# Ranks of tokens by a running sum on VectorE and three products, in place of nine products on TensorE

## The chip, the cores and the metric

The kernel runs on one core of a Trainium2 chip. The metric is device time in microseconds for one execution, the median of several runs; before the change it is 1121.83 us (three runs, 1119.72 to 1124.03).

## The reference

The input x is 128 graphs of 128 nodes with 128 features. Four layers follow one another, each a residual on a layer norm of x:

```python
x = x + gnn0(layernorm(x))   # h = x@W; softmax over neighbours of leaky_relu(s1_i + s2_j); elu(att @ h)
x = x + ffn0(layernorm(x))   # 8 experts, the best 2 of each token, softmax weights, gelu
x = x + gnn1(layernorm(x))   # as gnn0 with other weights; relu
x = x + ffn1(layernorm(x))   # 32 experts, the best 1 of each token, relu
```

For the two expert layers the tokens must be grouped. The first has 28 pairs of experts, the second 32 experts. Each token (a node of a graph) needs a row number: the start of its class, plus the tokens of that class in earlier batches, plus its rank in its own batch, which is how many tokens stand before it in the same class.

## The kernel before

There are two attention passes (l = 0 and 1), each followed by a mixture stage that reads the grouped tokens. A pass works in groups of G = 4 graphs, 32 groups (NG), as a software pipeline of turns `i`: in turn i group i is loaded and scaled, group i-1 gets its products h and scores, i-2 its weights, i-3 and i-4 the attention product, residual and statistics, i-5 its routing logits. The order of work in each engine is written out by hand in that engine's `graph_layer(l)`; engines meet in semaphores. VectorE's `link(op)` waits for the end of op before the next instruction; without it the next may start while op ends.

Routing and ranks are done for two groups at once. This is a batch b: eight graphs, w = 8 columns of tokens, 16 batches in each pass. On VectorE a turn runs, in this order: statistics of the coming x (first pass only), `weights` (L715, L722), in odd batches' turns `places`, `logits` (L754), then in the turn of a batch `first0`, `second0`, `pair0` (first pass, 28 pair codes) or `route1` (second pass, 32 experts), then `scores` (L742 the row maximum, L743 `nm`), `residual` (L732, L733 or L735, which write `staged`) and statistics. So in one turn of two the routing stands between `weights` and `scores`, and in the other turn `places` does.

The routing ends with a one-hot `oh` in bf16, of 8 x 28 = 224 or 8 x 32 = 256 elements a partition (L793, L800), with token columns outside and classes inside. A partition is a node number. The rank of a token is the count of ones of its class in all earlier graphs of the batch plus those on lower partitions of its own graph. TensorE makes that in the bank `SM`: one product with the strict triangle `below` (L1338), and eight with all ones (L1340), the q-th of which adds graph q to all the columns from q+1 on. The ninth column of the result is the batch's total. Then TensorE transposes `staged` (L1262), and makes h (L1279) and the scores (L1287, L1291, L1292) of a later group. In `places` (L809 to L829) VectorE adds the running `base`, multiplies by the one-hot and sums to the row numbers `dst`. GpSimd scatters the rows with them by indirect DMAs (L507), eight for each batch, and also computes the inverse deviations (L459, L469, L473). ScalarE's turn is: copies of `pt` (L1154) and `xT`, eight exponentials (L1117, L1118) that need `nm`, then the activations on the attention product, `x1T`, `xs_` and `hg`.

At the end of a pass a table of tiles is made from the counts, and the mixture stage starts when all scatters have landed.

Of the kernel before, what the change touches and what calls it, by code (L numbers as in the profile page):

```python
# [6 lines left out]
BF16 = mybir.dt.bfloat16  # L7
I32 = mybir.dt.int32
U32 = mybir.dt.uint32
ALU = mybir.AluOpType  # L10
# [3 lines left out]
P = 128  # L14
NGRAPH = 128
G = 4
# [71 lines left out]
def program(nc, x, adj, W_0, a_0, gamma, beta, Wr, br, W1_0, b1_0, W2_0, b2_0,  # L88
            W_1, a_1, rw, rb, W1_1, b1_1, W2_1, b2_1, out):
    with ExitStack() as ctx:  # L90
        def sb(name, shape, dt=F32):
            return ctx.enter_context(nc.sbuf_tensor(name, shape, dt))
# [29 lines left out]
        below = sb("below", [P, P], BF16)  # L122
        cmat = sb("cmat", [P, P])
        eps = sb("eps", [P, 2, 2 * G])
        eps1 = sb("eps1", [P, G])
# [83 lines left out]
        th = sb("th", [P, RB])  # L209
        ka = sb("ka", [P, RB])  # L210
        oh = sb("oh", [P, RB * NB[0]], BF16)
        base = [sb(f"base{s}", [P, E1]) for s in range(2)]
        pos = sb("pos", [P, RB * NB[0]])
        posoh = sb("posoh", [P, RB * NB[0]])
# [213 lines left out]
        def _(pool):  # L428
# [62 lines left out]
            pool.memset(onesb[:, :], 1.0).then_inc(sem("onesb"), 1)  # L491
            pool.memset(pad[:, :], 0.0).then_inc(sem("pad"), 1)
            pool.wait_ge(sem("onesb"), 1)
            pool.affine_select(out=below[:, :], in_=onesb[:, :], compare_op=ALU.is_gt, fill=0.0, base=0,
                               pattern=[[1, P]], channel_multiplier=-1)
            pool.wait_ge(sem("pad"), 1)
            pool.memset(pad[:, ID:ID + 1].bitcast(I32), NOWHERE).then_inc(sem("pad"), 1)

# [68 lines left out]
        def _(dve):  # L567
# [192 lines left out]
            def rows(t, k, E):  # L760
                return t[:, 0:E].unsqueeze(1).broadcast_to([P, k * G, E])

            def best(src, k, E, r, m, key):

                a, c = ge3(la, k, E), ge3(lk, k, E)
                link(dve.reduce_max(m[:, 0:k * G], src, AX.X))
                link(dve.tensor_tensor(a, src, wide(m, k, E), ALU.is_ge))
                link(dve.tensor_tensor(c, a, rows(r, k, E), ALU.mult))
                link(dve.reduce_max(key[:, 0:k * G], c, AX.X))
# [14 lines left out]
            def pair0(b, k):  # L784
                w = k * G
                mark(dve.tensor_tensor(ka[:, 0:w], k1[:, 0:w], k2[:, 0:w], ALU.add))
                dve.tensor_tensor(sd[:, 0:w], k1[:, 0:w], k2[:, 0:w], ALU.is_gt)
                after(dve, "th", b - 1)
                mark(dve.tensor_tensor(hd[:, 0:w], ma[:, 0:w], mb[:, 0:w], ALU.subtract))
                settled()  # L790
                dve.scalar_tensor_tensor(hd[:, 0:w], sd[:, 0:w], 0.5, hd[:, 0:w], ALU.subtract, ALU.mult).then_inc(sem("hd"), 1)
                after(dve, "rank_ps", b - 1)
                dve.tensor_tensor(ge3(oh, k, NB[0]), rows(codes, k, NB[0]), wide(ka, k, NB[0]), ALU.is_equal).then_inc(sem("oh"), 1)  # L793

            def route1(b, k):
                E = E1
                link(dve.tensor_tensor(ge3(lg, k, E), ge3(lgb, k, E), rows(cl[1], k, E), ALU.add))
                best(ge3(lg, k, E), k, E, rev, ma, k1)
                after(dve, "rank_ps", b - 1)
                dve.tensor_tensor(ge3(oh, k, E), rows(rev, k, E), wide(k1, k, E), ALU.is_equal).then_inc(sem("oh"), 1)  # L800

            def places(b):
                g, k = ORDER[b]
                l, w = g // NG, k * G
                B = NB[l]
                after(dve, "rank_ps", b)
                r = SM[:, 0:(w + 1) * B].rearrange("p (g e) -> p g e", e=B)
                old, new = base[b % 2], base[(b + 1) % 2]
                dve.tensor_tensor(new[:, 0:B], old[:, 0:B], r[:, w, :], ALU.add).then_inc(sem("base"), 1)  # L809
                dve.tensor_tensor(ge3(pos, k, B), r[:, 0:w, :], old[:, 0:B].unsqueeze(1).broadcast_to([P, w, B]),  # L810
                                  ALU.add).then_inc(sem("ranks_read"), 1)
                if l == 0:
                    after(dve, "th", b)
# [7 lines left out]
                        dve.tensor_scalar(staged[:, s:s + run, :, WHI], t, -0.5, 0.5, ALU.mult, ALU.add)  # L821
                        h += run
                after(dve, "ranks_read", b)
                link(dve.tensor_tensor(ge3(posoh, k, B), ge3(pos, k, B), ge3(oh, k, B), ALU.mult))
                if b >= ND:
                    for m in range(ORDER[b - ND][0], sum(ORDER[b - ND])):
                        dve.wait_ge(sem(f"scattered{m % NS}"), 16 * G * (m // NS + 1))
# [390 lines left out]
        def _(pe):  # L1218
# [46 lines left out]
            def graph_layer(l):  # L1265
                E = (E0, E1)[l]
                B = NB[l]
                for i in range(NG + 8):
# [62 lines left out]
                    if i in PART[l][2]:  # L1331
                        b = PART[l][2][i]
                        k = ORDER[b][1]
                        w = k * G
                        after(pe, "oh", b)
                        o = oh[:, 0:w * B].rearrange("p (g e) -> p g e", e=B)
                        r = SM[:, 0:(w + 1) * B].rearrange("p (g e) -> p g e", e=B)
# [115 lines left out]
```

## Time and profile before

| | us |
|---|---|
| median of 3 runs | 1121.83 |
| profiled execution, its own time | 1121.34 |
| its span, first to last instruction | 1119.6 |
| TensorE busy | 888.0 |
| VectorE busy | 794.6 |
| GpSimd busy | 761.7 |
| ScalarE busy | 699.1 |

The passes and the mixture stages follow one another, so a busy share has to be read within a stage. PEclk is the granted share of TensorE's full clock: 1.00 is 2.4 GHz, 0.50 is 1.2 GHz, and a value between is a mean over the stretch. A row of windows gives the stretch and its length, then for each engine the busy microseconds and, as (x105), the number of instructions. In rows of the timeline the first number is the start, the second the duration from the first to the last of the instructions merged in the row (their pipelined ends included), and the bracket gives how long the engine stood idle before and what ended it.

### The profile page before, as it was taken

Reading aid. Unit: us, or ns where it says so; the run is one execution under the profiler, and the core shown is the slowest. Engines: PE = TensorE matmul, PEld = TensorE weight load, DVE = VectorE, ACT = ScalarE, POOL = GpSimd, SP = SyncE. Lnnn points to the kernel's source line nnn. Section 1 sums busy time; section 2 is a strip of 40 time slices with the busy share of each in tenths; the row PEclk is TensorE's granted clock in tenths of the full one; section 3 lists DMA queues with packets and bytes.
Section 4 is the critical chain, followed back from the end, with each engine's and each line's share of the span. In section 5 each row is a group of like instructions: output and inputs, shape, how many; then the busy total and the mean of one; then the engine's idle time right before and its main releaser. Section 6 shows DMA issues by size and latency. Waiting matters only on the chain. (4 is left out here: it accounts for less than half of the span.)

```text
span 1119.6 us, 26953 instructions
## 1 busy us (share of the span) xinstructions
PE 888.0 (79%) x6709; PEld 797.9 (71%) x6709; DVE 794.6 (71%) x3521; ACT 699.1 (62%) x2364; POOL 761.7 (68%) x975
## 2 busy tenths in 40 slices
PE   4788988988618999999999759999999518878810
PEld 3567777877618999999999747888888406666610
DVE  7779899888846999999999716888888823422310
ACT  2799899888504665566556459999998306653300
POOL 3327777677762887877888811787878846777776
PEclk9899899889758999999999979999999659985555
DMA  8323432221157888887878321223221145433311
GB/s 197 54 83 123 141 123 85 70 58 47 35 114 198 210 208 209 210 208 206 213 204 207 94 67 29 74 84 85 79 78 50 41 104 146 117 99 104 90 33 38
DMA packets 144935, 129.21 MB, mean 115 GB/s; under 512 B 26552, under 2 KB 116541, under 8 KB 144785
## 3 DMA queue, kind: packets, MB, share of 16 engines
q1 hardware_dynamic: 124144, 91.94, 33.2%
q0 software_dynamic: 17760, 34.20, 9.0%
q10 hardware_dynamic: 2880, 1.35, 0.6%
q8 instruction: 60, 0.98, 0.4%
q14 instruction: 91, 0.74, 0.3%
HBM read 82.74 MB, written 47.48 MB: 116 GB/s over the span
## 5 line engine op out<-in xcount | busy, mean ns | idle before, releaser
L507 POOL DMA_INDIRECT xs<-staged,dst x256 | 258.1, 1008 | 77.2 <-issue 68.6
L1168 ACT ACTIVATE hT<-bank,wt 128x128 f32<-128x128 f32 x620 | 177.3, 368 | 130.9 <-PE bank L1383 114.6
L538 POOL DMA_INDIRECT x2d<-ob,xi x155 | 161.0, 1038 | 43.0 <-issue 28.7
L560 POOL DMA_INDIRECT out<-oq,xq x144 | 142.9, 992 | 58.4 <-issue 42.7
L1369 PE MATMUL bank<-xnT,wt 128*128 128x128 f32 x1240 | 166.0, 277 | 0.0
L1383 PE MATMUL bank<-w2s,hT 128*128 x1240 | 164.0, 275 | 0.7 <-DVE ob L1041 0.5
L1369 PEld LDWEIGHTS bank<-xnT,wt 128*128 128x128 f32 x1240 | 152.8, 194 | 0.1
L1383 PEld LDWEIGHTS bank<-w2s,hT 128*128 128x128 f32 x1240 | 150.9, 192 | 1.0 <-issue 1.0
L1117 ACT ACTIVATE p<-bank,nm 128x128 f32<-128x128 f32 x256 | 103.2, 403 | 27.0 <-DVE nm L743 27.0
L1118 ACT ACTIVATE p<-bank,nm 128x128 f32<-128x128 f32 x256 | 104.8, 410 | 0.0
L1131 ACT ACTIVATE rl<-bank,rinv 128x128 f32<-128x128 f32 x256 | 97.1, 453 | 3.1 <-DVE staged L735 3.1
L1068 DVE SCALAR_TENSOR_TENSOR oq<-bank,xq 128x512 f32<-128x512 f32 x36 | 24.9, 692 | 103.0 <-PE bank L1414 57.3
L715 DVE SCALAR_TENSOR_TENSOR pm<-p 128x128 f32<-128x128 f32 x256 | 61.7, 288 | 46.0 <-ACT p L1118 44.7
L1303 PEld LDWEIGHTS bank<-hg,pt 128*128 128x128 f32 x512 | 68.3, 195 | 29.0 <-issue 29.0
L1279 PE MATMUL bank<-wcat,xT 128*128 128x128 f32 x512 | 78.4, 303 | 7.5 <-DVE wa L644 3.9
L1291 PEld LDWEIGHTS bank<-wa,xT 128*128 128x128 f32 x512 | 75.7, 212 | 6.1 <-issue 2.4
L1279 PEld LDWEIGHTS bank<-wcat,xT 128*128 128x128 f32 x512 | 71.5, 216 | 9.6 <-ACT xT L1106 4.9
L1210 ACT ACTIVATE xnqT<-bank 128x512 f32<-128x512 f32 x36 | 21.5, 596 | 89.1 <-PE bank L1262 89.1
L1291 PE MATMUL bank<-wa,xT 128*128 128x128 f32 x512 | 74.6, 294 | 0.0
L1328 PEld LDWEIGHTS bank<-wrc,x1T 128*128 128x128 f32 x512 | 64.7, 198 | 7.7 <-ACT x1T L1136 5.5
L1328 PE MATMUL bank<-wrc,x1T 128*128 128x8 f32 (+1 forms) x512 | 64.8, 262 | 6.4 <-ACT x1T L1136 3.3
L742 DVE TENSOR_REDUCE nmax<-bank 128x4 f32<-128x512 f32 x64 | 43.8, 685 | 35.7 <-PE bank L1292 35.7
(250 smaller groups left out, 2203.3 us busy)
## 6 DMA issues: line engine op xcount, KB each, us to landing
wt<-wpd SPq DMA_DIRECT2D x155, 258.0 KB
xi<-xs SPq DMA_DIRECT2D x155, 66.0 KB
xq<-xs SPq DMA_DIRECT2D x144, 66.0 KB
xb<-x2d SPq DMA_DIRECT2D x32, 258.0 KB, 3.1
xb<-in_x SPq DMA_DIRECT2D x32, 256.0 KB, 3.9
wpd<-w1c SPq DMA_DIRECT2D x56, 129.0 KB
xs<-staged,dst POOLq DMA_INDIRECT x256, 2.5
x2d<-ob,xi POOLq DMA_INDIRECT x155
```

The lines of the kernel that those rows point to most:

```text
L507: pool.indirect_dma_start(out=xs[l], out_offset=bass.IndirectOffsetOnAxis(ap=dst[b % ND][:, c:c + 1], axis=0), in_=stag[s][:, q, 0:ROW], i ...
L538: pool.indirect_dma_start(out=x2d, out_offset=bass.IndirectOffsetOnAxis(ap=xi[t % NXI][:, ID:ID + 1].bitcast(U32), axis=0), in_=ob[:, t % ...
L560: pool.indirect_dma_start(out=orow, out_offset=bass.IndirectOffsetOnAxis(ap=xq[j % NXQ][:, q, ID:ID + 1].bitcast(U32), axis=0), in_=oq[j % ...
L1117: act.activation(p1[:, q, :], S[:, q, :], ACT.Exp, bias=nm[:, q:q + 1])
L1118: last = act.activation(p2[:, q, :], S[:, q, :], ACT.Exp, bias=nm[:, q:q + 1], scale=SLOPE[l])
L1131: last = act.activation(rl[:, q, :], z, ACT.Relu, scale=rinv[m % 3][:, q:q + 1])
L1168: last = act.activation(hT[t % 2][:, j, :], HID[t % 2][:, j, :], ACT.Gelu, bias=wt[t % NW][:, c:c + 1])
L1279: last = pe.matmul(HB[:, c], xT[:, c], wcat[l][:, :], start=(q == 0), stop=(q == G - 1), skip_group_check=True)
L1291: pe.matmul(S[:, c], xT[:, c], wa1[l][:, :], start=False, stop=False, skip_group_check=True)
L1328: last = pe.matmul(SM[:, LOGITS[l] + q * E:LOGITS[l] + (q + 1) * E], x1T[:, q * P:(q + 1) * P], wrc[l][:, :], start=(q == 0), stop=(q == G ...
L1369: last = pe.matmul(HID[t % 2][:, j, :], wt[t % NW][:, c:c + P], xnT[t % 2][:, :], start=(j == 0), stop=(j == 3), skip_group_check=True)
L1383: last = pe.matmul(to, hT[t % 2][:, 2 * h + c, :], w2s[:, bass.ds(e + c * E0 * P, P)], start=(h == 0 and c == 0), stop=(h == 1 and c == 1) ...
```

## The change

The one-hot is written with classes outside and the eight graphs inside. VectorE then makes a running sum over it, `state = gate * state + oh`, where `gate` is 0 at the first graph of every class and 1 elsewhere: `upto_` holds for each class and graph the ones on that partition in this graph and all earlier ones. One product with all ones sums that over the partitions; one with `lessone` (0 for lower partitions, -1 for the token's own and higher ones) takes away the tokens of its own graph at and above its partition; a third, over the last graph of each class, is the total. TensorE waits for "prefix", which the scan signals, in place of "oh". `places` reads the ranks and the one-hot with graphs eight elements apart. On GpSimd the constants change: `lessone` and `gate` in place of `below`, with three more memsets.

```diff
+            pool.memset(onesb[:, :], 1.0)
+            pool.memset(gate[:, :], 1.0)
+            pool.memset(lessone[:, :], 0.0).then_inc(sem("onesb"), 1)
...
-            pool.affine_select(out=below[:, :], in_=onesb[:, :], compare_op=ALU.is_gt, fill=0.0, base=0,
+            pool.affine_select(out=lessone[:, :], in_=lessone[:, :], compare_op=ALU.is_gt, fill=-1.0, base=0,
                                pattern=[[1, P]], channel_multiplier=-1)
+            pool.memset(gate[:, :].rearrange("p (e g) -> p e g", g=2 * G)[:, :, 0], 0.0).then_inc(sem("gate"), 1)
...
+            def eg3(t, k, E):
+                return t[:, 0:k * G * E].rearrange("p (e g) -> p g e", e=E)
+
+            def prefix(b, k, E):
+                if b == 0:
+                    dve.wait_ge(sem("gate"), 1)
+                dve.tensor_tensor_scan(upto_[:, 0:k * G * E], gate[:, 0:k * G * E], oh[:, 0:k * G * E], 0.0, ALU.mult,
+                                       ALU.add).then_inc(sem("prefix"), 1)
...
-                dve.tensor_tensor(ge3(oh, k, NB[0]), rows(codes, k, NB[0]), wide(ka, k, NB[0]), ALU.is_equal).then_inc(sem("oh"), 1)
+                link(dve.tensor_tensor(eg3(oh, k, NB[0]), rows(codes, k, NB[0]), wide(ka, k, NB[0]), ALU.is_equal))
+                prefix(b, k, NB[0])
...
-                dve.tensor_tensor(ge3(oh, k, E), rows(rev, k, E), wide(k1, k, E), ALU.is_equal).then_inc(sem("oh"), 1)
+                link(dve.tensor_tensor(eg3(oh, k, E), rows(rev, k, E), wide(k1, k, E), ALU.is_equal))
+                prefix(b, k, E)
...
-                r = SM[:, 0:(w + 1) * B].rearrange("p (g e) -> p g e", e=B)
+                r = SM[:, 0:w * B].rearrange("p (e g) -> p g e", e=B)
...
-                link(dve.tensor_tensor(ge3(posoh, k, B), ge3(pos, k, B), ge3(oh, k, B), ALU.mult))
+                link(dve.tensor_tensor(ge3(posoh, k, B), ge3(pos, k, B), eg3(oh, k, B), ALU.mult))
...
-                        after(pe, "oh", b)
...
-                        pe.matmul(r[:, 0:w, :], below[:, :], o, start=True, stop=False, skip_group_check=True)
-                        for q in range(w):
-                            last = pe.matmul(r[:, q + 1:w + 1, :], onesb[:, :], o[:, q:q + 1, :].broadcast_to([P, w - q, B]),
-                                             start=False, stop=(q == w - 1), skip_group_check=True)
-                        last.then_inc(sem("rank_ps"), 1)
+                        after(pe, "prefix", b)
+                        n_ = w * B
+                        ends = upto_[:, 0:n_].rearrange("p (e g) -> p e g", g=w)[:, :, w - 1]
+                        pe.matmul(SM[:, 0:n_], lessone[:, :], oh[:, 0:n_], start=True, stop=False, skip_group_check=True)
+                        pe.matmul(SM[:, 0:n_], onesb[:, :], upto_[:, 0:n_], start=False, stop=False, skip_group_check=True)
+                        pe.matmul(SM[:, n_:n_ + B], onesb[:, :], ends, start=False, stop=True,
+                                  skip_group_check=True).then_inc(sem("rank_ps"), 1)
```

## Rows read from the trace of the kernel before

**Rows 1.** The page: busy time of each engine over the span.

```profile
PE 888.0 (79%) x6709; PEld 797.9 (71%) x6709; DVE 794.6 (71%) x3521; ACT 699.1 (62%) x2364; POOL 761.7 (68%) x975
```

**Rows 2.** Windows: twelve batches of the first pass, twelve of the second.

```profile
core 0: us, PE busy (x) PEld busy (x) DVE busy (x) ACT busy (x) POOL busy (x), PEclk, DMA share, GB/s
76.52:276.86 200.34, 173.01 (x1246) 152.96 (x1245) 179.58 (x886) 178.65 (x593) 144.15 (x166) 0.91 0.31 93
697.17:860.59 163.42, 155.78 (x1239) 138.01 (x1238) 139.92 (x625) 151.66 (x481) 127.09 (x165) 1.00 0.27 75
```

**Rows 3.** Windows, one batch each, from one-hot to next one-hot.

```profile
76.52:92.50 15.98, 14.20 (x113) 12.41 (x113) 14.97 (x75) 15.98 (x54) 8.96 (x11) 1.00 0.38 118
...
125.16:143.16 18.00, 15.43 (x102) 13.41 (x101) 15.05 (x75) 14.52 (x50) 13.10 (x15) 0.81 0.39 119
143.16:158.77 15.61, 13.28 (x108) 11.80 (x107) 14.86 (x75) 14.96 (x50) 11.74 (x14) 1.00 0.44 138
158.77:175.37 16.60, 14.13 (x103) 12.46 (x102) 15.07 (x76) 14.55 (x50) 13.55 (x15) 0.90 0.41 129
...
192.19:209.14 16.95, 14.69 (x105) 13.03 (x104) 15.08 (x76) 14.82 (x50) 12.07 (x14) 0.90 0.22 64
...
778.88:792.49 13.61, 12.97 (x105) 11.49 (x105) 11.66 (x52) 12.63 (x41) 10.86 (x15) 1.00 0.30 81
```

**Rows 4.** Timeline of VectorE in the first pass.

```profile
209.14 0.38 DVE L793 TENSOR_TENSOR oh<-codes,ka 128x224 bf16<-128x224 f32 x1
209.44 0.68 DVE L742 TENSOR_REDUCE nmax<-bank 128x4 f32<-128x512 f32 x1
...
216.91 0.69 DVE L742 TENSOR_REDUCE nmax<-bank 128x4 f32<-128x512 f32 x1 [0.80 <-PE bank L1292]
```

**Rows 5.** Timeline of TensorE in the first pass.

```profile
209.58 0.27 PE L1338 MATMUL bank<-oh,below 128*128 128x224 bf16 x1
209.69 0.61 PE L1340 MATMUL bank<-oh,onesb 128*128 128x224 bf16 x8
211.71 1.00 PE L1262 MATMUL bank<-ident,staged 128*128 128x128 f32 x4 [1.42 <-DVE staged L733]
```

**Rows 6.** VectorE's groups by form: count, busy us, mean ns, idle before.

```profile
L767 DVE TENSOR_TENSOR la<-lg,ma 128x256 f32<-128x256 f32 x16 | 6.8, 425 | 0.5
L766 DVE TENSOR_REDUCE ma<-lg 128x8 f32<-128x256 f32 x16 | 6.7, 420 | 0.5
...
L767 DVE TENSOR_TENSOR la<-lg,ma 128x64 f32<-128x64 f32 x16 | 3.6, 224 | 0.5
```

**Rows 7.** Timeline of VectorE in the second pass.

```profile
788.83 0.29 DVE L715 SCALAR_TENSOR_TENSOR pm<-p 128x128 f32<-128x128 f32 x1 [1.09 <-ACT p L1118]
...
792.04 0.42 DVE L769 TENSOR_REDUCE k<-lk 128x8 f32<-128x256 f32 x1
792.49 0.42 DVE L800 TENSOR_TENSOR oh<-rev,k 128x256 bf16<-128x256 f32 x1
792.84 0.68 DVE L742 TENSOR_REDUCE nmax<-bank 128x4 f32<-128x512 f32 x1
```

**Rows 8.** Timelines of TensorE and ScalarE in the second pass.

```profile
792.97 0.28 PE L1338 MATMUL bank<-oh,below 128*128 128x256 bf16 x1
794.38 0.66 PE L1262 MATMUL bank<-ident,staged 128*128 128x128 f32 x4 [0.62 <-DVE staged L735]
785.64 0.60 ACT L1154 ACTIVATE pt<-bank 128x512 f32<-128x512 f32 x1 [0.17 <-PE bank L1262]
793.75 0.37 ACT L1117 ACTIVATE p<-bank,nm 128x128 f32<-128x128 f32 x1 [0.80 <-DVE nm L743]
```

**Rows 9.** Timelines at the ends of the passes, and GpSimd's waits (us, times, longest).

```profile
296.64 0.20 POOL L459 TENSOR_TENSOR ve<-var,eps 128x4 f32<-128x4 f32 x1 [0.29 <-DVE var L619]
...
POOL xs L507 <- DVE dst L829: 8.1, 13, 1.5
...
912.50 0.96 POOL L507 DMA_INDIRECT xs<-staged,dst  x1 [0.30 <-issue]
```

More of the change, by code:

```diff
@@ L121, in program @@
         onesb = sb("onesb", [P, P], BF16)
-        below = sb("below", [P, P], BF16)
+        lessone = sb("lessone", [P, P], BF16)
+        gate = sb("gate", [P, RB // 2 * E1], BF16)
         cmat = sb("cmat", [P, P])
@@ L211, in program @@
         oh = sb("oh", [P, RB * NB[0]], BF16)
+        upto_ = sb("upto_", [P, RB * NB[0]], BF16)
         base = [sb(f"base{s}", [P, E1]) for s in range(2)]
@@ L490, in _ @@
             last.then_inc(sem("iotas"), 1)
-            pool.memset(onesb[:, :], 1.0).then_inc(sem("onesb"), 1)
+            pool.memset(onesb[:, :], 1.0)
+            pool.memset(gate[:, :], 1.0)
+            pool.memset(lessone[:, :], 0.0).then_inc(sem("onesb"), 1)
             pool.memset(pad[:, :], 0.0).then_inc(sem("pad"), 1)
             pool.wait_ge(sem("onesb"), 1)
-            pool.affine_select(out=below[:, :], in_=onesb[:, :], compare_op=ALU.is_gt, fill=0.0, base=0,
+            pool.affine_select(out=lessone[:, :], in_=lessone[:, :], compare_op=ALU.is_gt, fill=-1.0, base=0,
                                pattern=[[1, P]], channel_multiplier=-1)
+            pool.memset(gate[:, :].rearrange("p (e g) -> p e g", g=2 * G)[:, :, 0], 0.0).then_inc(sem("gate"), 1)
             pool.wait_ge(sem("pad"), 1)
@@ L806, in places @@
                 after(dve, "rank_ps", b)
-                r = SM[:, 0:(w + 1) * B].rearrange("p (g e) -> p g e", e=B)
+                r = SM[:, 0:w * B].rearrange("p (e g) -> p g e", e=B)
                 old, new = base[b % 2], base[(b + 1) % 2]
-                dve.tensor_tensor(new[:, 0:B], old[:, 0:B], r[:, w, :], ALU.add).then_inc(sem("base"), 1)
-                dve.tensor_tensor(ge3(pos, k, B), r[:, 0:w, :], old[:, 0:B].unsqueeze(1).broadcast_to([P, w, B]),
+                dve.tensor_tensor(new[:, 0:B], old[:, 0:B], SM[:, w * B:(w + 1) * B], ALU.add).then_inc(sem("base"), 1)
+                dve.tensor_tensor(ge3(pos, k, B), r, old[:, 0:B].unsqueeze(1).broadcast_to([P, w, B]),
                                   ALU.add).then_inc(sem("ranks_read"), 1)
@@ L1334, in graph_layer @@
                         w = k * G
-                        after(pe, "oh", b)
-                        o = oh[:, 0:w * B].rearrange("p (g e) -> p g e", e=B)
-                        r = SM[:, 0:(w + 1) * B].rearrange("p (g e) -> p g e", e=B)
-                        pe.matmul(r[:, 0:w, :], below[:, :], o, start=True, stop=False, skip_group_check=True)
-                        for q in range(w):
-                            last = pe.matmul(r[:, q + 1:w + 1, :], onesb[:, :], o[:, q:q + 1, :].broadcast_to([P, w - q, B]),
-                                             start=False, stop=(q == w - 1), skip_group_check=True)
-                        last.then_inc(sem("rank_ps"), 1)
+                        after(pe, "prefix", b)
[5 more added lines that the diff above has]
+                                  skip_group_check=True).then_inc(sem("rank_ps"), 1)
                     if 0 <= i - 4 < NG:
```

## The prediction

> **What bounds the kernel now.** The page's busy line first [rows 1]: no engine is above 79% of the span, so a share over everything decides nothing. The windows by stage then show where the edit lives [rows 2]. In the first attention pass, from 76.5 to 276.9 us, VectorE is busy 90% (179.58 of 200.34), ScalarE 89%, TensorE 86%. In the second pass's full part, 697.2 to 860.6 us, TensorE is busy 95%, ScalarE 93%, VectorE 86%. Read by shares alone, the second pass looks like TensorE's, and taking products from TensorE looks like a gain. The order in time says something else.
>
> A batch is eight graphs, two turns of the pipeline, 16 batches in each pass. In the second pass every batch takes 13.6 us (the last of [rows 3]). Follow one turn round [rows 7, 8]: ScalarE ends the exponentials, and VectorE, which had waited 1.09 us for them, starts L715 at 788.83. From there it never stops: masked weights, logits, `route1`, the one-hot at 792.49, the row maximum at 792.84, `nm`. ScalarE has waited 0.80 us for that `nm`, and runs from 793.75 until the next such L715. From 788.83 to 793.75 the loop is VectorE's, 4.9 us; the other 8.7 of the batch's 13.6 us are ScalarE's. TensorE stands beside it: it starts the rank products at 792.97, and then waits 0.62 us for `staged`, which VectorE writes after `nm`. So the products fill time in which TensorE would wait.
>
> In the first pass a batch takes 15.61 to 15.98 us where the granted clock is 1.00 (three batches of twelve), 16.60 to 16.95 us in eight and 18.00 us in one [rows 3]. The rank products start at 209.58 and TensorE then waits 1.42 us for `staged` [rows 5]. VectorE comes to that `staged` straight through routing, one-hot and row maximum; behind it, TensorE's work at half clock makes VectorE wait 0.80 us in the next turn's L742 [rows 4]. Where the clock is full, VectorE alone sets the batch.
>
> **Removed: TensorE's products.** Columns per batch fall from 224 + (8+7+...+1) x 28 = 1232 to 224 + 224 + 28 = 476 in the first pass, from 1408 to 544 in the second. One column is 1/2.4 ns at full clock; [rows 5] agree, the nine products taking 0.72 us for 1232 columns with the last one's tail (0.51 us without). That is 0.32 and 0.36 us less a batch. I book it at nothing: the waits of 1.42 and 0.62 us stand right behind. If that cover were gone the edit would give back 0.32 x 14 + 0.36 x 13 = 9.2 us.
>
> **Added: a completed one-hot and a running sum on VectorE.** (a) The one-hot is now followed by a wait for its end. Unlinked, a 256-element instruction starts its successor 0.35 us later (792.49 to 792.84); linked, 0.46 us (792.04 to 792.49). Plus 0.11 us. At 224 elements the unlinked pitch is 0.30 (209.14 to 209.44), so 0.41 linked [rows 4, 7]. (b) The scan over 224 or 256 elements. No row shows one. From below: it costs what a tensor_tensor of that size does, a pitch of 0.30 or 0.35 us. From above: each element waits for two dependent operations (multiply by the gate, then add), so an element takes two steps in place of one. From 64 to 256 elements an instruction grows from 224 to 425 ns, 1.04 ns an element [rows 6]; the second step adds 0.23 us (224) or 0.27 us (256): pitches of 0.53 and 0.61 us. I take the upper. The reduction, nearest of all rows, does feed each result into the next and runs at one element a step (420 ns at 256), but it has one operation in its loop, the scan two.
>
> Together VectorE does 0.64 us more a batch in the first pass and 0.73 us in the second, before `nm`, `staged` and everything queued behind. TensorE waits longer behind "prefix": its queue holds the transposes of `staged`, which are late anyway by the same amount; ScalarE waits longer for `nm`.
>
> The Trainium skill, page "DVE: opcode table, instruction layouts, handler registers and perf-mode slots", section "Datapath and trigger behaviour", says that the built-in running sum sends its result back to an earlier stage and runs at half throughput. That speaks against this change; by it the sum is the upper one, and by the reduction's row the lower, 6.7 us less. No run here shows it yet.
>
> (c) Edits at nothing. `places` now reads PSUM and the one-hot eight elements apart (L810, L824). If each element took two steps this would add 0.46 to 0.54 us, but in the second pass 1.09 us of waiting for ScalarE follows in that turn, and in the first the 0.80 us wait for TensorE; it shows only in batches at full clock. Writing the one-hot at that stride (L793, L800) is on the path; 0 from below, 0.23 or 0.27 us from above. Every row of a wide instruction here has contiguous output and none is nearer to one end; I take 0, since it still writes one element a step, and keep the other end for the range. GpSimd's three more memsets of at most 256 elements come once, some 65 us ahead of the first batch; at VectorE's 0.4 us for 256 elements they would be 1 us of a stretch in which GpSimd mostly waits: 0. The rows before the pass, the mixture stages and all DMAs are untouched.
>
> **How many batches count.** At each pass's end GpSimd's scatters take over. In the first, its last wait for VectorE's statistics is the 0.29 us at 296.64, after the one-hot of the fourteenth batch; from there it runs without waiting for VectorE until the last scatter. In the second, GpSimd waits for `dst` 13 times, the last for the thirteenth batch, then works through to 912.50 [rows 9]. What VectorE loses in later batches is hidden behind that queue. In the last batch of a pass nothing but the products stands between one-hot and `places`, and the edit could gain; that too is hidden. So 14 x 0.64 + 13 x 0.73 = 9.0 + 9.5 = 18.5 us.
>
> **TensorE's clock.** In the first pass it fell to half in nine of the twelve batches from 76.52 to 276.86 us; batches without a fall average 15.8 us and all twelve 16.7 us [rows 2, 3], so the falls cost 0.9 us a batch (200.34 / 12 - 15.8). What stood before them is the 1.42 us gap, with little but narrow products ahead of it. In the second pass, gap 0.62 us, the mean is 1.00 over twelve batches [rows 2]. After the change TensorE runs out of work at 793.0 as now, gets the prefix about 793.65 (792.49 + 0.46 + 0.69), works about 0.3 us, and waits for `staged` until 795.1: gaps of 0.65 and 1.15 us with a short burst between, together more than the 1.42 us that went with falls. A fall costs more there, since TensorE's way from `staged` to the transposed weights ends with ScalarE waiting 0.17 us for it [rows 8]: 3 to 4 us of work at half clock is up to 1.7 us, of which I count 1.1. I take half of 13 batches: 7 us. In the first pass the gaps grow to 0.6 and 1.9 us; if nearly every batch falls and one in six falls twice (18.00 us, plus 2.2), the mean is 1.3 in place of 0.9: 0.4 x 12 = 5 us. Both are estimates from these rows.
>
> The Trainium skill, "TensorE: Matmul & The Clock Gate", section "Part 1: The HAM clock gate", says that the default is the throttled state and that activity releases it. The trace agrees at the 0.90 rows, and by that rule taking work from TensorE beside a wait costs twice.
>
> **The sum** against the profiled execution, 1121.34 us (span 1119.6; the median is 1121.83): 18.5 + 7 + 5 = 30.5, so 1152 us.
>
> **Rivals.** *Work only* (chance 0.22): the clock behaves as now, 1121.3 + 18.5 = 1140 us. For: in the first pass 1.4 us gaps also went by without a fall (three batches). *Full-rate sum* (0.14): the scan streams like the reduction; 14 x 0.41 + 13 x 0.46 = 11.7, so 1133 us without clock losses, 1143 with most of them. *More than one loss* (0.13): strided writes at two steps (14 x 0.23 + 13 x 0.27 = 6.7) or falls in nearly every batch of the second pass (13 x 1.1 = 14 in place of 7): 1159 to 1166 us. *The other side* (0.05): TensorE is the bound after all. It holds if the products end later than `staged`, that is if the 0.62 us wait is only apparent and VectorE's additions fit in its own 0.32 and 1.09 us waits: then 1121.3 - 9.2 = 1112 us, or about 1121 if both cancel. Against it: the added work stands after those waits, not before them, and ScalarE's 0.80 us wait is for VectorE. My forecast, 0.46, has its own range of 1144 to 1159 us. A measurement of this kernel tells about 0.5% (5.6 us) from no change; only the last rival, 0.02 faster and 0.03 same, stays inside or below that, and with it 0.01 more of the full-rate case. The range for 8 in 10 reaches from just below the full-rate case to the larger losses, 1131 to 1165 us.
>
> **What the profile after would show.** The scan's row: near 620 and 690 ns (upper) or 384 and 424 ns (lower). From the one-hot's start to L742's: 0.94 and 1.07 us in place of 0.30 and 0.35. A batch of the second pass at 14.3 us where the clock is 1.00 and near 15.5 where it fell; TensorE's two gaps; L1117's wait for `nm` longer, L715's 1.09 us unchanged or shorter. GpSimd's wait for `dst` grows by 0.7 us in each of 13 batches. The mixture stages keep their length. The prediction is wrong if TensorE's granted clock stays 1.00 in the second pass, if the scan takes as long as a tensor_tensor, or if the batch does not grow by what VectorE gained.

## The result, and the profile after

The changed kernel takes 1197.78 us (median of four runs, 1194.77 to 1200.60) against 1122.63 us for the kernel before in the same comparison (1119.72 to 1124.03): 1.0668 times, 95% interval 1.0644 to 1.0692. The direction was forecast, the size was not: 30 us were expected and 75 came, and the forecast's range, up to 1165 us, does not hold it. The profiled execution took 1198.69 us (span 1196.7, mean granted clock 0.845), 77.1 us of span more than before.

The page of the changed kernel: span, busy time by engine, and the granted clock in forty slices.

```profile
span 1196.7 us, 26605 instructions
...
PE 918.9 (77%) x6517; PEld 819.0 (68%) x6517; DVE 848.7 (71%) x3553; ACT 697.8 (58%) x2364; POOL 769.3 (64%) x978
...
PEclk9888988888657999999999699988998755797555
```

VectorE is busy 54 us longer than in [rows 1]. TensorE is busy 31 us longer too, though it has 192 products fewer, with a mean granted clock of 0.845 where it was 0.881. In the slices of the first pass (the third to the twelfth) the granted clock is mostly 0.8; a 9 stands for anything from 0.90 up, so the second pass is read from its windows below.

Its groups by form in the first pass (100 to 280 us; count, busy us, mean ns, idle before), then both forms of the one-hot and of the sum from a query by tile (min/median/max ns):

```profile
L807 DVE TENSOR_TENSOR oh<-codes,ka 128x224 bf16<-128x224 f32 x9 | 10.3, 1143 | 0.0
L840 DVE TENSOR_TENSOR posoh<-pos,oh 128x224 f32<-128x224 f32 x10 | 5.7, 566 | 0.0
L774 DVE TENSOR_TENSOR_SCAN upto_<-gate,oh 128x224 bf16<-128x224 bf16 x9 | 5.6, 625 | 0.3
L826 DVE TENSOR_TENSOR pos<-bank,base 128x224 f32<-128x224 f32 x10 | 3.8, 383 | 0.0
```

```profile
L774 DVE TENSOR_TENSOR_SCAN upto_<-gate,oh x32: 624/658/692, 76.5 to 964.6; 128x224 bf16<-128x224 bf16 x16, 128x256 bf16<-128x256 bf16 x16
...
L815 DVE TENSOR_TENSOR oh<-rev,k x16: 1290/1294/1298, 726.4 to 963.3; 128x256 bf16<-128x256 f32 x16
```

The sum takes 624 and 692 ns, the forecast's upper price (near 620 and 690). The one-hot is the surprise: 1144 ns in place of 384 and 1294 in place of 424 [rows 4, 7]. Its elements and its arithmetic are the same; what changed is that neighbours in the loop are now written 8 elements apart. That is 0.76 and 0.87 us a batch, where the prediction had 0 and, as its upper bound, 0.23 and 0.27.

Windows of one batch each, two of the first pass and two of the second (start:end, length, busy time and count of PE, PEld, DVE, ACT, POOL, granted clock, DMA share, GB/s):

```profile
150.05:169.35 19.30, 15.42 (x99) 13.36 (x98) 16.60 (x76) 14.76 (x50) 12.64 (x14) 0.82 0.36 112
169.35:187.58 18.23, 14.34 (x99) 12.50 (x98) 16.64 (x76) 14.77 (x50) 12.20 (x14) 0.91 0.38 118
827.31:844.16 16.85, 14.32 (x100) 12.33 (x99) 13.50 (x53) 12.61 (x41) 11.07 (x14) 0.90 0.23 65
844.16:859.40 15.24, 12.71 (x100) 11.10 (x99) 13.47 (x54) 12.66 (x41) 9.86 (x13) 1.00 0.26 66
```

Set these beside [rows 3]. The last row is the batch without a fall: 15.24 against 13.61 + 0.73 (link and sum) + 0.87 (one-hot) = 15.21. The row above it is what eleven of the twelve full batches look like: a fall of the clock, a stretch at half clock, adds 1.6 us to them. In the first pass the two rows alternate, one fall and two, and none is free of one.

The timeline of one routing in the second pass, VectorE and TensorE (start, us, what it waited for):

```profile
793.62 1.30 DVE L815 TENSOR_TENSOR oh<-rev,k 128x256 bf16<-128x256 f32 x1
...
794.95 0.69 DVE L774 TENSOR_TENSOR_SCAN upto_<-gate,oh 128x256 bf16<-128x256 bf16 x1
795.55 0.67 DVE L747 TENSOR_REDUCE nmax<-bank 128x4 f32<-128x512 f32 x1
...
795.69 0.28 PE L1354 MATMUL bank<-oh,lessone 128*128 128x256 bf16 x1 [1.60 <-DVE upto_ L774]
...
796.45 0.37 ACT L1133 ACTIVATE p<-bank,nm 128x128 f32<-128x128 f32 x1 [2.42 <-DVE nm L748]
...
797.08 0.66 PE L1278 MATMUL bank<-ident,staged 128*128 128x128 f32 x4 [0.94 <-DVE staged L740]
```

From the one-hot's start to the row maximum it is 1.93 us where [rows 7] have 0.35. ScalarE's wait for `nm` grew from 0.80 [rows 8] to 2.42 us, by the 1.6 us that VectorE gained. TensorE has two gaps, 1.60 and 0.94 us with 0.4 us of work between, where it had one of 0.62.

GpSimd's waits in the second pass (720 to 990 us; us, times, longest):

```profile
POOL xs L512 <- DVE dst L845: 21.9, 14, 1.7
```

[Rows 9] had 8.1 us.

**Where the 77.1 us lie.** The starts of the first one-hot of each pass are 75.31 and 726.40 us (76.52 and 697.17 before), the starts of the last scatters 358.95 and 984.15 us (331.41 and 912.50). So the first pass grew by 28.7 us (283.6 after, 254.9 before), the stretch between by 1.7, the second pass by 42.4 (257.8 after, 215.3 before), the last stage by 5.5, and 1.2 came off the start.

### The profile page after: what moved, and what is told of

Its sections match the earlier page's. It is cut to its first block and busy times, and to the rows that moved or that the text cites. A ratio compares the mean times of both kernels' runs of the same rounds, so it can differ in the third digit from the quotient of the medians.

```text
span 1196.7 us, 26605 instructions
## 1 busy us (share of the span) xinstructions
PE 918.9 (77%) x6517; PEld 819.0 (68%) x6517; DVE 848.7 (71%) x3553; ACT 697.8 (58%) x2364; POOL 769.3 (64%) x978
## 3 DMA queue, kind: packets, MB, share of 16 engines
q10 hardware_dynamic: 2880, 1.35, 0.6%
## 5 line engine op out<-in xcount | busy, mean ns | idle before, releaser
L512 POOL DMA_INDIRECT xs<-staged,dst x256 | 265.1, 1036 | 90.9 <-issue 67.8
L565 POOL DMA_INDIRECT out<-oq,xq x144 | 144.6, 1004 | 62.2 <-issue 42.4
L1133 ACT ACTIVATE p<-bank,nm 128x128 f32<-128x128 f32 x256 | 101.8, 398 | 64.8 <-DVE nm L748 64.7
L1134 ACT ACTIVATE p<-bank,nm 128x128 f32<-128x128 f32 x256 | 103.4, 404 | 0.0
L1295 PE MATMUL bank<-wcat,xT 128*128 128x128 f32 x512 | 90.2, 335 | 6.6 <-ACT xT L1122 3.6
L1307 PEld LDWEIGHTS bank<-wa,xT 128*128 128x128 f32 x512 | 85.3, 235 | 7.8 <-issue 2.4
L1295 PEld LDWEIGHTS bank<-wcat,xT 128*128 128x128 f32 x512 | 83.0, 246 | 8.7 <-ACT xT L1122 4.9
L1307 PE MATMUL bank<-wa,xT 128*128 128x128 f32 x512 | 82.8, 315 | 0.0
L1278 PE MATMUL bank<-ident,staged 128*128 128x128 f32 x256 | 51.7, 336 | 36.7 <-DVE staged L738 23.7
L461 POOL TENSOR_TENSOR ve<-var,eps 128x8 f32<-128x8 f32 (+1 forms) x38 | 8.6, 226 | 107.3 <-DVE var L624 107.3
L1170 ACT ACTIVATE pt<-bank 128x512 f32<-128x512 f32 x64 | 42.2, 660 | 56.1 <-PE bank L1278 56.0
```

Of the source, the lines that this page charges most:

```text
L512: pool.indirect_dma_start(out=xs[l], out_offset=bass.IndirectOffsetOnAxis(ap=dst[b % ND][:, c:c + 1], axis=0), in_=stag[s][:, q, 0:ROW], i ...
L565: pool.indirect_dma_start(out=orow, out_offset=bass.IndirectOffsetOnAxis(ap=xq[j % NXQ][:, q, ID:ID + 1].bitcast(U32), axis=0), in_=oq[j % ...
L1133: act.activation(p1[:, q, :], S[:, q, :], ACT.Exp, bias=nm[:, q:q + 1])
L1134: last = act.activation(p2[:, q, :], S[:, q, :], ACT.Exp, bias=nm[:, q:q + 1], scale=SLOPE[l])
L1295: last = pe.matmul(HB[:, c], xT[:, c], wcat[l][:, :], start=(q == 0), stop=(q == G - 1), skip_group_check=True)
L1307: pe.matmul(S[:, c], xT[:, c], wa1[l][:, :], start=False, stop=False, skip_group_check=True)
```

## The experiments

Four of them (`after_fill`, `probe_strides`, `e1_late`, `b_fill_order`) ran on a chip on which the kernel before takes 1177.13 us, with longer mixture stages (in `b_fill_order` 380 us between the passes and 249 behind the last scatter, where the kernel before has 366 and 207); from these only ratios, batches, lengths of the passes and durations are used.

**1. The one-hot in memory order.** All of the change, but the loop of the one-hot runs as its result lies in memory; its inputs are broadcasts either way.

```diff
-link(dve.tensor_tensor(eg3(oh, k, E), rows(rev, k, E), wide(k1, k, E), ALU.is_equal))
+link(dve.tensor_tensor(eg(oh, k, E), deep(rev, k, E), wided(k1, k, E), ALU.is_equal))
+# eg:    [0:k*G*E] as "p (e g) -> p e g";  deep: class value, broadcast over g;  wided: key, broadcast over e
```

> The changed kernel with one thing undone: the one-hot is computed in the order in which it lies in memory (class by class, the eight graphs innermost), so each write is next to the last; its values and its place are the same. Theory A (the stride of the 16-bit write is what I priced at 0): the one-hot falls from 1144 and 1294 ns to 384 and 424 ns, VectorE's path by 0.76 and 0.87 us a batch, 14 x 0.76 + 13 x 0.87 = 22 us: 1176 us if the clock falls as often as in the changed kernel, 1152 us if in half of the second pass's batches, 1140 us if as in the kernel before. Rival B (the operands with a broadcast in the middle, or the waits, make it slow, not the stride): the one-hot stays above 1 us and the time near 1198 us.

1159.87 us (1156.99 to 1160.48), 1.0306 times the kernel before (1.0273 to 1.0340). The one-hot is back at 384 and 424 ns. Of twelve batches in the second pass, seven are like the first of these windows and five like the second:

```profile
726.28:740.65 14.37, 12.71 (x100) 11.11 (x99) 12.61 (x53) 12.67 (x41) 9.46 (x13) 1.00 0.28 71
740.65:756.63 15.98, 14.28 (x100) 12.55 (x99) 12.64 (x54) 12.60 (x41) 12.42 (x16) 0.89 0.25 72
```

This is the kernel that the prediction described: 14.3 us forecast for a batch at full clock, a fall in about half of the batches. Writing without the stride gives back 38 us, half of the whole loss; that holds the write's own time and the falls that it drew. Still, the time is 8 us above the 1152 expected for this case. Of these, 5 lie in the last stage (212.1 us behind the last scatter, 207.1 before), which had been booked at nothing.

**2. Products that nobody reads, behind the prefix.** The version of 1, with 14 (first pass) and 8 (second) products of ones into `SM`, which the rank products then overwrite.

```diff
 after(pe, "prefix", b)
+for _ in range(FILL[l]):
+    pe.matmul(SM[:, 0:224]..., onesb[:, :], onesb[:, 0:112].unsqueeze(1).broadcast_to([P, 2, 112]), start=True, stop=True)
```

> As the kernel with the contiguous one-hot, plus products on ones that nobody reads (224 columns each; 14 a batch in the first pass, 8 in the second), which TensorE does between the arrival of the prefix and the rank products, in the time in which it would wait for staged. They leave the result as it is. Theory of the clock (falls follow from TensorE's gap and cost 1.1 to 1.6 us a batch): granted clock 1.00 in all batches, second pass 14.35 us a batch, first pass about 16.3: 1121 + 18.5 - 11 = 1129 us. Rival (the clock's falls are hidden, or come anyway): the same time as without the added products, or longer by their 1.3 and 0.75 us a batch where these end after staged.

1144.29 us (1142.36 to 1151.07), ratio 1.0196 (1.0150 to 1.0242). In the second pass all batches take 14.37 us at a granted clock of 1.00:

```profile
759.55:773.92 14.37, 13.44 (x108) 11.83 (x107) 12.59 (x54) 12.62 (x41) 11.21 (x15) 1.00 0.28 76
210.03:226.61 16.58, 14.12 (x111) 12.47 (x111) 15.79 (x77) 14.77 (x49) 11.99 (x15) 1.00 0.23 66
```

TensorE does more, and the kernel is faster. In the first pass only some batches are free of falls (the second row), others take 17.0 us at 0.90, and the 1129 us expected with no fall anywhere is missed.

**3. The sum without the removal.** The kernel before, its layout and its nine products, but the one-hot is linked and followed by a sum that nobody reads, and the nine products wait for it. The rival is that taking the products away is what opened the gaps.

```diff
-...is_equal).then_inc(sem("oh"), 1)
+link(...is_equal)); dve.tensor_tensor_scan(upto_, oh, oh, 0.0, mult, add).then_inc(sem("prefix"), 1)
-after(pe, "oh", b)
+after(pe, "prefix", b)
```

> The kernel before with VectorE's additions alone: the wait for the one-hot's end and a running sum of the same size, whose result nobody uses; the nine products stay and wait for it. Layout and one-hot as before. If taking the six products away matters through the clock (theory C), the clock here stays as before and the time is 1121 + 18.5 = 1140 us, less than the contiguous kernel. If VectorE's longer path alone makes the gaps (theory D), the time equals the contiguous kernel's within 0.5%.

1158.59 us (1157.42 to 1159.45), ratio 1.0303 (1.0271 to 1.0334): the same as experiment 1, with nine products in place of three. A batch with a fall:

```profile
725.27:741.22 15.95, 14.64 (x105) 13.02 (x105) 12.43 (x53) 12.61 (x41) 12.55 (x16) 0.89 0.25 72
```

Four of twelve batches of the second pass fall here, five in experiment 1. So in these two kernels six products fewer a batch are worth nothing that shows, neither as time saved nor as a clock lost, and VectorE's longer way makes the whole difference. The rival fell.

**4. The kernel before, filled.** Eight unread products ahead of the nine, first pass only; nothing else changed.

> The kernel before with 8 products on ones that nobody reads (224 columns each, about 0.75 us) ahead of the rank products of every batch of the first pass, in the time of the 1.42 us wait for staged. Theory of the clock: no falls in the first pass, a batch at 15.6 to 15.8 us in place of 16.7: 1121 - 12 = 1110 us. Rival (falls are hidden behind VectorE, or come anyway): 1121 us, at most 0.5% away.

1109.22 us (1108.84 to 1110.20), ratio 0.9865 (0.9836 to 0.9895), faster than both kernels. The full batches of the first pass take 15.7 us (the first of them 15.98) where [rows 3] have 16.6 to 18.0 in nine of twelve:

```profile
201.29:217.01 15.72, 13.85 (x112) 12.30 (x112) 14.96 (x75) 14.77 (x50) 12.38 (x15) 1.00 0.23 70
```

The falls of the clock in the first pass cost the kernel before 12.8 us (from its first one-hot to its last scatter 254.9 us, here 242.1), and they can be bought off with work that has no use.

**5. The changed kernel, filled behind the prefix only.**

> The changed kernel with the strided one-hot, plus the same unread products (14 and 8 a batch) between the arrival of the prefix and the rank products. If the falls of the clock come from TensorE's gap ahead of staged alone, they vanish: second pass 14.37 + 0.87 = 15.2 us a batch in place of 16.84, first pass 16.58 + 0.76 = 17.3 in place of 18.8: 1198 - 20 - 17 = 1161 us. If the longer gap ahead of the prefix (1.3 us and more, which these products cannot fill) is enough for a fall, most batches stay at 0.90 and the time gains less than 10 us: above 1188 us.

1235.15 us, ratio 1.0494 (1.0459 to 1.0529). In the second pass three of twelve batches take 15.24 us at 1.00 and nine 16.45 to 16.84 us at 0.90. The time lies between the two that were expected (1161 us and above 1188; 1.0494 times 1122.63 is 1178). Filling one of the two gaps does a part; with the one ahead of the prefix left, 1.3 to 1.6 us, most batches still fall. What filling both does is experiment 10.

**6. What a stride costs.** The kernel before, with 19 VectorE instructions ahead of its end, each linked, nothing of theirs used: the same 256-element comparison with a 16-bit output at 1, 2, 4, 8 and 16 elements apart, with a 32-bit output at 1, 2, 4 and 8, then reads 8 apart from 16-bit, 32-bit and PSUM operands, writes of a whole block in strided order (one of them of 128 elements), then sums.

> The kernel before, with single VectorE instructions of 256 elements at the end of VectorE's work, each waiting for the one ahead: a comparison written in 16 bits with the elements 1, 2, 4, 8 and 16 apart; in 32 bits 1, 2, 4 and 8 apart; a product that reads a 16-bit, a 32-bit or a PSUM operand 8 apart; comparisons that write the whole block in strided order; sums over 256 and 64 elements, and one in 32 bits. Theory A1 (a write costs more when the next one leaves its 16 bytes): 16-bit at 8 and 16 apart near 1290 ns, 32-bit at 4 and 8 apart near 1290 too, the closer ones 424. Rival A2 (only parts of a 32-bit word are dear): every 16-bit write with a stride of 2 or more is near 1290 ns, every 32-bit one at 424. The 16-bit read 8 apart near 645 ns; the sums 690 and 290 ns at two steps an element.

One execution, 1180.12 us. The timeline of VectorE (start, us); L1086 to L1090 are the 16-bit outputs, L1091 (not shown, 0.42) to L1094 the 32-bit ones, L1096 the read of the 16-bit one-hot and L1098 of PSUM, L1100 a write of 128 16-bit elements 8 apart, L1102 the sum:

```profile
1164.65 0.42 DVE L1086 TENSOR_TENSOR w2s<-pos,posoh 128x256 bf16<-128x256 f32 x1
1165.10 0.45 DVE L1087 TENSOR_TENSOR w2s<-pos,posoh 128x256 bf16<-128x256 f32 x1
1165.58 0.77 DVE L1088 TENSOR_TENSOR w2s<-pos,posoh 128x256 bf16<-128x256 f32 x1
1166.39 1.29 DVE L1089 TENSOR_TENSOR w2s<-pos,posoh 128x256 bf16<-128x256 f32 x1
1167.71 1.23 DVE L1090 TENSOR_TENSOR w2s<-pos,posoh 128x256 bf16<-128x256 f32 x1
...
1169.43 0.42 DVE L1092 TENSOR_TENSOR w2s<-pos,posoh 128x256 f32<-128x256 f32 x1
1169.89 0.61 DVE L1093 TENSOR_TENSOR w2s<-pos,posoh 128x256 f32<-128x256 f32 x1
1170.54 0.62 DVE L1094 TENSOR_TENSOR w2s<-pos,posoh 128x256 f32<-128x256 f32 x1
...
1171.65 0.61 DVE L1096 TENSOR_TENSOR w2s<-posoh,oh 128x256 f32<-128x256 f32 x1
...
1172.94 0.42 DVE L1098 TENSOR_TENSOR w2s<-posoh,bank 128x256 f32<-128x256 f32 x1
...
1174.72 0.72 DVE L1100 TENSOR_TENSOR oh<-posoh 128x128 bf16<-128x128 f32 x1
...
1176.14 0.69 DVE L1102 TENSOR_TENSOR_SCAN w2s<-oh 128x256 bf16<-128x256 bf16 x1
```

16-bit writes cost 0.42, 0.45, 0.77, 1.29 and 1.23 us; 32-bit writes 0.42, 0.42, 0.61 and 0.62; reads of SBUF 8 apart 0.61 to 0.62; reads of PSUM 8 apart nothing. Neither theory was whole: the cost grows with the stride, as one had it, but at 8 elements apart a 16-bit write is twice as dear as a 32-bit one (1.29 and 0.62). Bytes apart alone don't explain it (16-bit at 8 and 32-bit at 4 are both 16 bytes apart: 1.29 and 0.61).

The Trainium skill, page "SBUF — State Buffer", section "Specifications (TRN2)", speaks of 16-byte lines that want two accesses each for full bandwidth. By that rule 16-bit writes 4 apart would be free; measured they are not (0.77), and at 8 apart, a new line for each, the slowdown is there (1.29).

**7. The sum out of VectorE's way to `nm` and `staged`.** The version of 1, with the sum behind `staged` on VectorE and the three products behind the transposes of `staged` on TensorE.

> The kernel with the contiguous one-hot, with the running sum moved behind staged on VectorE and the three products behind the transposes of staged on TensorE, so that neither nm nor staged waits for the sum. If the sum costs time because it stands ahead of nm and staged, the second pass (where VectorE waits 1.4 us a batch for ScalarE) loses most of the 0.61 us: about 13.9 us a batch, and TensorE's gaps shrink, so few falls; the first pass, where VectorE is the bound, stays near 16.6 to 17.5: about 1143 us. Rival (VectorE's work costs its length wherever it stands): 1160 us, as with the sum ahead.

1203.37 us, ratio 1.0215 (1.0186 to 1.0245), against 1.0306 in experiment 1 on the other chip. In the second pass batches take 14.2 us at 1.00 and 15.85 at 0.89, little less than before the move (14.37 and 15.98); the expected 13.9 is missed. From first one-hot to last scatter the passes take 264.9 and 232.1 us, in experiment 1 268.9 and 235.9, so the move gives back 8 us where 17 were expected. TensorE now has one gap in place of two:

```profile
825.78 0.66 PE L1290 MATMUL bank<-ident,staged 128*128 128x128 f32 x4 [1.50 <-DVE staged L740]
```

The falls stay with a single gap of 1.5 us: five of twelve batches, as in experiment 1.

**8. Routing behind `nm` in the filled kernel before.** In the second pass `scores` comes ahead of `route1` on VectorE. If ScalarE's wait for `nm` [rows 8] is the hinge of a batch, this shortens it.

```diff
+if 0 < i - 1 < NG: scores(n - 1)
 if i in PART[1][0]: route1(b, ORDER[b][1])
-if 0 < i - 1 < NG: scores(n - 1)
```

> The kernel before with unread products in the first pass (1109 us), and in the second pass the routing and one-hot behind the row maximum and nm in place of ahead of them. By my reading of the second pass's loop (ScalarE, then VectorE's routing, then nm) ScalarE no longer waits for the routing: a batch falls from 13.6 towards TensorE's 13.0 busy, about 13.2: 1109 - 13 x 0.4 = 1104 us. Rival (staged, not nm, is what the loop hangs on, and it stays as late as now): 13.6 us a batch and 1109 us, or a little more where the rank products now end after staged.

1175.64 us, ratio 0.9977 (0.9961 to 0.9994), worse than 0.9865 without it. The first pass is as long as in experiment 4 (242.1 us), the second takes 225.1 us in place of 215.2. Its batches take 14.2 us, not 13.6, and two of twelve fall. The waits from 700 to 870 us (us, times, longest):

```profile
PE bank L1343 <- DVE oh L801: 13.8, 11, 1.4
ACT pt L1155 <- PE bank L1263: 12.9, 10, 1.6
```

ScalarE no longer waits for `nm`, but it waits up to 1.6 us for TensorE's transposes, where [rows 8] have 0.17. TensorE in turn waits for the one-hot, which now comes later and stands ahead of `staged` in its queue. So an earlier `nm` makes nothing faster here. That the batch is VectorE's work and then ScalarE's was too narrow a reading of the second pass: TensorE's way from the one-hot through `staged` is about as long. This order delays the one-hot as well, so it does not tell `staged` from the one-hot as the hinge.

**9. The layout without sum and link.** The kernel before with only the one-hot transposed: a strided write, strided reads by `places` and by all nine products.

> The kernel before with the layout of the one-hot alone changed: classes outside and graphs inside, written and read eight elements apart, the nine products kept, no running sum and no wait for the one-hot's end. VectorE's path grows by the stride's 0.76 and 0.87 us a batch. If a batch costs what VectorE does ahead of staged plus a fall of the clock in some batches, this is like the contiguous kernel, whose path grew by 0.64 and 0.73 us: second pass 14.5 us a batch at clock 1.00 and near 16.1 where it fell, ratio to the kernel before 1.03 to 1.04. Rival (the stride and the running sum cost together more than each alone, through something other than the clock): 1.02 or less here. TensorE's strided reading could add to the products' 0.7 us, which a wait of 1.4 us hides.

1184.98 us (1177.88 to 1187.10), ratio 1.0535 (1.0498 to 1.0572), more than the 1.03 to 1.04 expected. TensorE pays for the stride too, as its timeline in the second pass shows:

```profile
791.07 0.61 PE L1341 MATMUL bank<-oh,below 128*128 128x256 bf16 x1 [0.85 <-DVE oh L803]
791.50 2.23 PE L1343 MATMUL bank<-oh,onesb 128*128 128x256 bf16 x8
793.55 1.08 PE L1265 MATMUL bank<-ident,staged 128*128 128x128 f32 x4
```

The first product takes 0.61 us where [rows 8] have 0.28, and the next work starts 2.48 us after it in place of 1.41, now delaying the transposes: the products are no longer hidden. Every batch of the second pass falls (16.55 to 17.12 us at 0.90), though TensorE's only gap is 0.85 us; the falls stand behind two microseconds of slow, strided streaming. In the changed kernel the two wide products read what lies contiguous, and it doesn't pay this.

**10 to 12. Both gaps filled.** The changed kernel and the version of 1, with unread products also ahead of the logits' products, in the time before the prefix comes; and the changed kernel as it is beside them.

```diff
+for _ in range(FIRST[l] if i in PART[l][2] else 0):   # (12, 14) and (6, 7)
+    pe.matmul(SM[:, 0:224]..., onesb[:, :], onesb[:, 0:112].unsqueeze(1).broadcast_to([P, 2, 112]), start=True, stop=True)
 for q in range(G): last = pe.matmul(SM[...], x1T, wrc[l], ...)
```

> The changed kernel, with unread ones-products of 224 columns in both of TensorE's gaps of a batch: 12 (first pass) and 14 (second) ahead of the logits' products, that is in the 1.3 to 1.6 us before the prefix comes, and 14 and 8 behind the prefix. If what the strided one-hot and the sum put on VectorE is 18.5 + 22 = 40.5 us and all the rest of the loss is the clock, every batch runs at a granted clock of 1.00: 15.2 us in the second pass, about 17.1 in the first, and the kernel is at the filled kernel before plus that, 0.9865 + 40.5 / 1122 = 1.023 times the kernel before (1.02 to 1.03). If something else in the change costs time, the batches are longer than these at full clock and the ratio stays above 1.04.

> The version with the one-hot written in memory order, with unread products in both gaps (6 and 7 ahead of the logits' products, 14 and 8 behind the prefix). If only VectorE's sum and link are left, the first pass too is at full clock throughout, 16.4 us a batch, the second at 14.4, and the ratio is 0.9865 + 18.5 / 1122 = 1.003 (1.00 to 1.01); with the fillers behind the prefix alone it was 1.0196. If the products ahead delay the logits, the batches grow instead and it stays at 1.02.

> The changed kernel as it is, on the same chip as the two filled ones, to have all three beside the same runs of the kernel before: 1.067 times the kernel before, with falls of the clock in ten of eleven batches of the second pass.

The changed kernel: 1198.40 us as it is (ratio 1.0631, 1.0601 to 1.0661; ten of twelve batches of the second pass fall), 1162.14 us filled (1.0314, 1.0290 to 1.0338). The contiguous version filled: 1136.51 us (1.0094, 1.0067 to 1.0122). One full batch of each pass of the filled changed kernel; from the first batch of a pass to the twelfth all are at 1.00:

```profile
217.91:235.27 17.36, 15.29 (x125) 13.63 (x124) 16.57 (x77) 14.81 (x49) 12.05 (x15) 1.00 0.21 63
...
804.60:819.86 15.26, 14.79 (x122) 13.17 (x120) 13.47 (x54) 12.64 (x41) 10.83 (x15) 1.00 0.27 72
```

So at least 36 us of the changed kernel's time is the clock. One batch pays for the filling, the first of the first pass. Its prefix is there before TensorE comes to it, so the unread products fill no wait, `staged`'s transposes start late, and VectorE waits for the scores of the next turn:

```profile
77.54:96.38 18.84, 16.58 (x137) 14.85 (x137) 16.58 (x76) 17.73 (x59) 9.40 (x11) 1.00 0.31 100
...
87.21 0.69 DVE L749 TENSOR_REDUCE nmax<-bank 128x4 f32<-128x512 f32 x1 [1.14 <-PE bank L1310]
```

This batch is 2.86 us longer than in experiment 4 (15.98), the next ones 1.62, so the filling costs 1.2 us. Both ratios are 0.6 to 0.8% above the sums expected: the last stage, `places` and the count of batches, in the terms below, were not in those sums.

## Why the prediction was wrong

**What bounds the kernel: held.** The batch grows by what VectorE gains ahead of `nm`, to 0.03 us in the second pass (15.24), and the products saved are worth nothing (experiment 3). Only the finer reading, that `nm` is the hinge and TensorE stands beside it, did not hold (experiments 7 and 8).

**The sum and the link: held.** 624 and 692 ns, and 14.37 us a batch in experiment 1 against 13.61 + 0.73 = 14.34.

The Trainium skill says that this built-in sum runs at half throughput (page "DVE: opcode table, instruction layouts, handler registers and perf-mode slots", section "Datapath and trigger behaviour"). The trace agrees: from 64 to 256 elements the sum grows from 0.29 to 0.69 us (experiment 6), 2.1 ns an element, where [rows 6] have 1.04.

**The step that failed: "I take 0, since it still writes one element a step".** The strided write of the one-hot takes 0.76 and 0.87 us a batch more, three times the upper bound. The bound was itself a guess in disguise: no wide row of the trace had a strided output, and "two steps at most" was carried over from the sum, where two dependent operations gave a reason for it. From 128 to 256 elements the strided comparison grows by 0.57 us (0.72 to 1.29), 4.5 ns an element (L1100 and L1089 in experiment 6), where contiguous ones take 1.04 [rows 6].

**The clock: right in kind, then multiplied by that error.** With a contiguous write, falls came in five of twelve batches of the second pass (forecast: half) at 1.6 us (forecast 1.1). The stride lengthened TensorE's wait for the prefix from 0.75 to 1.60 us, and then nearly every batch fell. To size it, compare filled with unfilled kernels from a pass's first one-hot to its last scatter. Changed kernel: 283.6 against 266.0 in the first pass, 257.8 against 239.0 in the second. With the 1.2 us that the filling itself costs in the first pass, 18.8 and 18.8 us lie in falls. Kernel before: 12.8 and 0.1. The net is 6.0 us in the first pass (forecast 5) and 18.7 in the second (forecast 7).

When the clock falls stays open. The length of TensorE's wait does not tell it alone. In twelve batches of the second pass the runs have no fall with one wait of 0.62 us (before), four with 0.70 and 0.60 (experiment 3), five with 0.72 and 0.94 (experiment 1), five with one of 1.5 to 1.6 (experiment 7), two with one of 0.85 to 1.4 (experiment 8), eleven with 1.60 and 0.94 (the changed kernel) and twelve with one of 0.85 beside slow products (experiment 9). What is shown is that products in these waits keep the clock up.

**How many batches count: right in the first pass, too few in the second.** Filled kernels differ by 1.62 us a batch in the first pass (17.35 to 15.73) and 1.64 in the second (15.25 to 13.61), and by 23.9 and 23.7 us from first one-hot to last scatter. Less the 1.2 us of the filling, that is 14.0 batches in the first pass, as forecast, and 14.45 in the second, in place of 13. GpSimd's wait for `dst` shows it: 14 waits and 21.9 us there, where [rows 9] have 13. The queue of scatters hides less of the last batches when each is later.

**`places`: as bounded.** Its strided read of the one-hot costs 0.19 us (L840, 566 ns against 378 before the change), hidden in the second pass and paid in the first at full clock, as forecast. Its PSUM read costs nothing (L826, 383 ns).

**The last stage, booked at nothing, gives 5.5 us.** GpSimd's stores of the changed kernel begin at 1000.27 us; the fifth waits for `oq`. Two rows of it, then the fifth store of the kernel before:

```profile
1004.15 0.98 POOL L565 DMA_INDIRECT out<-oq,xq  x1 [0.31 <-issue]
1008.82 0.97 POOL L565 DMA_INDIRECT out<-oq,xq  x1 [3.69 <-DVE oq L1084]
...
933.40 0.97 POOL L560 DMA_INDIRECT out<-oq,xq  x1 [0.62 <-issue]
```

That is 3.1 of the 5.5 us; the first store comes 0.7 us later behind the last scatter (16.1 us, before 15.4), and 1.7 are not traced. In the kernel before TensorE is at full clock by the second tile of the stage (eight products in 1.06 us at 926.33), here still at half (1.91 us at 998.67). The same wait of 3.7 us stands in experiments 1 and 3. Why the clock comes back a tile later there was not tested.

The terms beside each other, in us of the profiled span:

| term | forecast | measured |
|---|---|---|
| link and sum | 18.5 | 14.0 x 0.64 + 14.45 x 0.73 = 19.5 |
| strided write | 0 (to 6.7) | 14.0 x 0.76 + 14.45 x 0.87 = 23.2 |
| `places` and remainder of a batch | 0 | 14.0 x 0.22 + 14.45 x 0.04 = 3.7 |
| clock, first pass | 5 | 6.0 |
| clock, second pass | 7 | 18.7 |
| last stage | 0 | 5.5 |
| start, and between the passes | 0 | 0.5 |
| sum | 30.5 | 77.1 |

The counts of batches and the remainders were worked out from the lengths of the passes, so the sum has to close; the prices of the instructions, the clock's terms and the last stage are read from the traces.

The rivals: *work only* and *full-rate sum* are excluded by the falls and by the sum's row. *More than one loss* named both mechanisms that did it, the stride and falls in nearly every batch, and ended at 1166 because the first was capped at 0.23 us and the two were not allowed to feed each other. *The other side* has nothing for it.

## What to carry to other kernels

Before a layout is transposed so that one reader gets it contiguous, price the write: here a 16-bit result written 8 elements apart cost three times its time, and looping in the order of memory undid it at no cost. Waits like TensorE's here, 0.6 to 1.6 us in every batch, are worth reading beside its granted clock, and filling them with products that nobody reads made the kernel before 1.35% faster; of the changed kernel's 1198 us it gave back 36. When no row of the trace shows a form of access, the bound of its cost must be a wide one, and a loss that lengthens a wait of TensorE is to be carried into the clock's term as well.

## What the hardware showed that was not expected

VectorE, 256 elements: 16-bit writes at 1, 2, 4, 8, 16 elements apart take 0.42, 0.45, 0.77, 1.29 and 1.23 us, 32-bit writes 0.42, 0.42, 0.61, 0.62 (1, 2, 4, 8), SBUF reads 8 apart 0.61 to 0.62, PSUM reads 8 apart 0.42. TensorE streams a 16-bit operand 8 elements apart in 0.61 us where the contiguous one takes 0.28 (256 columns), and its clock fell in every batch of the second pass with such streaming and a gap of only 0.85 us.
